# Attention on one Trainium2 core: GpSimd finishes q's rope ahead of k's, and makes the next head's lower weight parts in the waits of that order

## The chip, the cores and the metric

The kernel runs on one core of one Trainium2 chip. The metric is device time in microseconds (us) of one execution. The kernel before takes 2588.76 us, the median of three runs (2585.17 to 2589.17).

## The reference

The program is one transformer block in float32: a layer norm, an attention with three branches, a residual, and a feed-forward layer that routes 128 tokens per batch. The change lies in the attention, which is for each of 16 heads and 8 batches (512 tokens, head width 128):

```
q = (x @ Wq).reshape(b, n, H, HD)
k = (x @ Wk).reshape(b, n, H, HD)
v = (x @ Wv).reshape(b, n, H, HD)
q = _rope(q)
k = _rope(k)
...
return jnp.concatenate([t1 * cos - t2 * sin, t1 * sin + t2 * cos], axis=-1)
...
s_full = jnp.einsum('bnhd,bmhd->bhnm', q, k) * scale
```

The rope multiplies each half of q and k by a cosine and adds the other half times a signed sine. Compressed, selected and windowed softmax branches then share the scores of q and k.

## The kernel before

The attention (`attend`) goes through 128 units, one for a head and a batch; unit u is head u // 8 and batch u % 8. It is a software pipeline written by hand: in one pass of `body`, each engine projects unit u, scores unit u-1 and ends unit u-2 (the product of probabilities and v). Products keep float32 precision by splitting each operand into a high part (a copy rounded by ScalarE) and a low part (the difference), with three matmuls for one.

Every engine has one instruction stream in program order and waits on semaphores. In a unit:

- TensorE projects q and k (L479), scores the unit before (L505, L508), transposes probabilities (L521), projects v (L479 again), transposes v (L535) and multiplies by v (L546). Before it projects k it waits until ScalarE has copied the v of the unit before (`vt`) out of the bank that both share.
- ScalarE copies the projected q and k out of PSUM into `s_full` (L563), makes `pt_hi` (L579), then q's high part (L574), the exponentials of rows 3 and 2 (L585, L591), k's high part (L574), the exponentials of rows 1 and 0, and then `vt` (L563), `o_sb` (L625) and `v_hi` (L628). In the last unit of a head it also makes the high parts of the next head's weights (L134).
- SyncE stores `o_sb` (L405), and for q and then k swaps the two halves of `s_full` into `s_swap` with two DMAs (L396, L397). In the first unit of a head it also issues, behind that unit's store, the three weight loads of the next head (L130).
- GpSimd does the rope of q and k on 128x512 tiles. `turn_cos` (L440) is `s_full` times cosine, into `cosed`, once the copy is there. `turn_sin` waits for both swap DMAs, multiplies `s_swap` by sine (L445) and adds `cosed` and `s_swap` into `s_full` (L448). `low` (L452) takes the low part, once ScalarE has made the high part. The weights' low parts (L138) are made in the same stream, in the last unit of each head.
- VectorE reads score rows, works out the softmax coefficients and mixes the branches.

The inner loop `with eng.Fori(0, B - 1)` runs seven of a head's units; the unit with the weight split is written out ahead of it.

Of the kernel before, what the change touches and what calls it, by code (L numbers as in the profile page):

```python
# [84 lines left out]
def f32(ap):  # L85

    return ap.bitcast(F32)
# [215 lines left out]
def attend(nc, phase, banks, m, gates, xt_hi, xt_lo, weights, rope_d, o_dram, chunks):  # L303
# [68 lines left out]
    def steps(eng, body, start=lambda h: None, spare=lambda: None):  # L372


        start(0)
        body(0, 0, True, False, False, False)
        body(1, 1, True, True, False, False)
        with eng.Fori(2, B - 1) as b:
            body(b, b, True, True, True, False)
        with eng.Fori(1, H) as h:  # L380
            body(h * B - 1, B - 1, True, True, True, h)
            start(h)
            with eng.Fori(0, B - 1) as b:
                body(h * B + b, b, True, True, True, False)
        body(H * B - 1, B - 1, True, True, True, False)
        body(H * B, None, False, True, True, False)
        spare()
        body(H * B + 1, None, False, False, True, False)

    with nc.Block() as block:  # L390
# [45 lines left out]
        @block.gpsimd  # L436
        def _(pool):
            def turn_cos(u, k):
                pool.wait_ge(evacuated[k], u + 1)
                nc.gpsimd.tensor_tensor(cosed[k][:], s_full[k][:], rope[:, 0, :], ALU.mult).then_inc(cos_done[k], 1)  # L440

            def turn_sin(u, k):

                pool.wait_ge(swapped[k], u * 32 + 32)
                nc.gpsimd.tensor_tensor(s_swap[k][:], s_swap[k][:], rope[:, 1, :], ALU.mult).then_inc(sin_done[k], 1)  # L445
                pool.wait_ge(cos_done[k], u + 1)
                pool.wait_ge(sin_done[k], u + 1)
                nc.gpsimd.tensor_tensor(s_full[k][:], cosed[k][:], s_swap[k][:], ALU.add).then_inc(roped[k], 1)  # L448

            def low(u, k):  # L450
                pool.wait_ge(hi_done[k], u + 1)
                nc.gpsimd.tensor_tensor(qk_lo[k][:], s_full[k][:], f32(qk_hi[k][:]), ALU.subtract).then_inc(lo_done[k], 1)  # L452

            def body(u, b, project, score, end, split):
                if project:
                    for k in range(2):
                        turn_cos(u, k)
                        if split is not False:
                            weights.low(pool, nc.gpsimd, split, k)
                    for part in (turn_sin, low):  # L460
                        for k in range(2):
                            part(u, k)
                    if split is not False:
                        weights.low(pool, nc.gpsimd, split, 2)

            nc.gpsimd.memset(o_sb[:], 0.0).then_inc(out_slot_free, 16)
            nc.gpsimd.memset(shift1[:], 0.0).then_inc(out_evacuated, 1)
            pool.wait_ge(rope_loaded, 16)
            steps(pool, body, spare=lambda: chunks.low(pool, 0, 0, 1))

        @block.tensor
# [973 lines left out]
```

## Time and profile before

| what | value |
|---|---|
| median of three runs | 2588.76 us |
| the profiled execution's own time | 2585.8 us |
| its span, from first to last instruction | 2584.0 us |
| mean granted TensorE clock, as a share of full | 0.980 |
| TensorE busy (share of the span) | 2453.7 us (95%) |
| VectorE | 1843.8 us (71%) |
| GpSimd | 1590.1 us (62%) |
| ScalarE | 1412.9 us (55%) |

A busy share is an average over stages. The attention takes roughly the stretch from 120 us to 1965 us. What an order of instructions does there shows in the timeline of each engine: the start of one instruction minus the start of the one before it is the pace at which they follow, and brackets give how long the engine was idle before it and what ended that.

### The profile page before, as it was taken

The numbers are of one execution on the slowest core, as the hardware profiler recorded it, in microseconds if no ns is written. First come the engines' busy times: TensorE is split into PE (matmuls) and PEld (weight loads), VectorE is DVE, ScalarE is ACT, GpSimd is POOL, SyncE is SP. The second block draws the span as 40 slices with busy tenths as digits, with TensorE's granted clock in tenths as the row PEclk, the third lists the DMA queues.
The fourth block names the chain that finished last, engine by engine and source line by source line (L and its number), as shares of the span: only waits on it lengthen the run. The fifth ranks groups of instructions, "written<-read, shape, count | busy, mean of one in ns | idle before, by whom it ended". The sixth has DMA issues, their size and how long they took to land. (4 is left out here: it accounts for less than half of the span.)

```text
span 2584.0 us, 48592 instructions
## 1 busy us (share of the span) xinstructions
PE 2453.7 (95%) x12944; PEld 2082.9 (81%) x12944; DVE 1843.8 (71%) x5891; ACT 1412.9 (55%) x3810; POOL 1590.1 (62%) x1177
## 2 busy tenths in 40 slices
PE   5799999999999999999999999999996999999998
PEld 4688888888888888888888888888885888887776
DVE  6378888787787888778788878778883566566134
ACT  6466666666665666566666666656663222222442
POOL 0367777777777777677777767777762343343442
PEclk9899999999999999999999999999998999999999
DMA  3222222221212121222222222121215343342366
GB/s 119 65 53 66 61 61 61 61 73 49 71 50 72 50 73 53 69 61 61 61 61 64 57 64 70 50 70 50 61 53 178 118 143 125 119 146 70 103 179 208
DMA packets 145629, 211.74 MB, mean 82 GB/s; under 512 B 14912, under 2 KB 56128, under 8 KB 144576
## 3 DMA queue, kind: packets, MB, share of 16 engines
q1 hardware_dynamic: 145600, 211.37, 27.6%
q8 instruction: 16, 0.26, 0.0%
q14 instruction: 13, 0.11, 0.0%
HBM read 93.87 MB, written 50.33 MB: 56 GB/s over the span
## 5 line engine op out<-in xcount | busy, mean ns | idle before, releaser
L479 PE MATMUL bank<-xt_hi,w_hi 128*128 (+1 forms) x1536 | 630.4, 410 | 43.8 <-ACT vt L563 40.0
L479 PE MATMUL bank<-xt_hi,w_lo 128*128 (+1 forms) x1536 | 607.6, 396 | 0.0
L479 PE MATMUL bank<-xt_lo,w_hi 128*128 (+1 forms) x1536 | 605.3, 394 | 0.0
L440 POOL TENSOR_TENSOR cosed<-s_full,rope 128x512 f32<-128x512 f32 x256 | 329.8, 1291 | 371.1 <-ACT s_full L563 369.5
L479 PEld LDWEIGHTS bank<-xt_hi,w_hi 128*128 128x128 f32 x1536 | 293.1, 191 | 108.9 <-ACT vt L563 46.7
L641 DVE TENSOR_REDUCE shift<-bank 128x1 f32<-128x512 f32 (+3 forms) x512 | 247.9, 484 | 158.7 <-PE bank L508 158.7
L448 POOL TENSOR_TENSOR s_full<-cosed,s_swap 128x512 f32<-128x512 f32 x256 | 331.2, 1294 | 36.7
L445 POOL TENSOR_TENSOR s_swap<-s_swap,rope 128x512 f32<-128x512 f32 x256 | 329.4, 1287 | 39.2 <-DMA s_swap<-s_full 39.2
L479 PEld LDWEIGHTS bank<-xt_hi,w_lo 128*128 128x128 f32 x1536 | 292.4, 190 | 66.6
L479 PEld LDWEIGHTS bank<-xt_lo,w_hi 128*128 128x128 f32 x1536 | 293.9, 191 | 52.7
L452 POOL TENSOR_TENSOR qk_lo<-s_full,qk_hi 128x512 fp32r<-128x512 f32 x256 | 324.8, 1291 | 0.3 <-ACT qk_hi L574 0.3
L579 ACT ACTIVATE pt_hi<-bank 128x384 fp32r<-128x384 f32 (+1 forms) x384 | 174.6, 528 | 250.2 <-PE bank L521 250.2
L791 POOL TENSOR_TENSOR o_lo<-o_raw,o_hi 128x2048 fp32r<-128x2048 f32 x32 | 147.2, 4601 | 254.2 <-ACT o_hi L902 204.5
L563 ACT ACTIVATE s_full<-bank 128x512 f32<-128x512 f32 x256 | 154.5, 603 | 262.0 <-PE bank L479 261.8
L574 ACT ACTIVATE qk_hi<-s_full 128x512 fp32r<-128x512 f32 x256 | 160.4, 626 | 171.9 <-POOL s_full L448 171.9
L645 DVE TENSOR_REDUCE bank<-bank 128x8 f32<-128x512 f32 (+3 forms) x512 | 253.2, 495 | 0.0
L585 ACT ACTIVATE bank<-bank,shift 128x512 f32<-128x512 f32 (+3 forms) x512 | 251.3, 491 | 1.1 <-DVE bank L645 1.0
L591 ACT ACTIVATE win<-win,shift 128x192 f32<-128x192 f32 (+1 forms) x512 | 222.9, 435 | 0.0
L964 PE MATMUL bank<-wo_hi,o_hi 128*128 128x512 f32 x512 | 204.9, 400 | 6.1 <-PEq L390 3.3
L658 DVE SCALAR_TENSOR_TENSOR bank<-bank,coef,cb 128x192 f32<-128x192 f32 (+1 forms) x512 | 206.9, 404 | 0.0
L650 DVE TENSOR_TENSOR pt_lo<-bank,pt_hi 128x384 fp32r<-128x384 f32 (+1 forms) x384 | 206.2, 593 | 0.9 <-ACT pt_hi L579 0.8
L674 DVE SCALAR_TENSOR_TENSOR probs<-win,coef,bank 128x192 f32<-128x192 f32 (+1 forms) x512 | 199.9, 390 | 4.5
(164 smaller groups left out, 5429.2 us busy)
## 6 DMA issues: line engine op xcount, KB each, us to landing
s_swap<-s_full SPq DMA_DIRECT2D x512, 128.0 KB, 2.3
o_scratch<-o_sb SPq DMA_DIRECT2D x128, 256.0 KB, 2.0
o_raw<-o_scratch SPq DMA_DIRECT2D x32, 1024.0 KB, 6.4
xin<-in_L_attn_x SPq DMA_DIRECT2D x16, 1024.0 KB, 5.4
w_raw<-in_L_ffn_W SPq DMA_DIRECT2D x64, 256.0 KB, 3.1
base_scratch<-x SPq DMA_DIRECT2D x8, 1024.0 KB, 4.7
base<-base_scratch SPq DMA_DIRECT2D x32, 256.0 KB, 4.3
out<-base SPq DMA_DIRECT2D x32, 256.0 KB, 2.6
```

Source lines behind the costliest of these rows:

```text
L440: nc.gpsimd.tensor_tensor(cosed[k][:], s_full[k][:], rope[:, 0, :], ALU.mult).then_inc(cos_done[k], 1)
L445: nc.gpsimd.tensor_tensor(s_swap[k][:], s_swap[k][:], rope[:, 1, :], ALU.mult).then_inc(sin_done[k], 1)
L448: nc.gpsimd.tensor_tensor(s_full[k][:], cosed[k][:], s_swap[k][:], ALU.add).then_inc(roped[k], 1)
L452: nc.gpsimd.tensor_tensor(qk_lo[k][:], s_full[k][:], f32(qk_hi[k][:]), ALU.subtract).then_inc(lo_done[k], 1)
L479: last = nc.tensor.matmul(banks[QB[k]][:, :], w[k][:, c, :], v[:, bass.ds(b, 1), c, :], start=(n == 0), stop=(n == 3 * C - 1))
L585: nc.scalar.activation(n, n, ACT.Exp, bias=shift1[:, t:t + 1], scale=-1.0, accum_out=sums[:, 1, t:t + 1]).then_inc(exp_row, 1)
L591: nc.scalar.activation(win[:, t, lo:], win[:, t, lo:], ACT.Exp, bias=shift2[:, t:t + 1], scale=-1.0, accum_out=sums[:, 2, t:t + 1]).then_i ...
L641: nc.vector.tensor_reduce(shift1[:, t:t + 1], n[:, 0:(t + 1) * P], AX.X, ALU.min)
L645: nc.vector.reduce_sum(sc[:, t, 0:nb], n[:, 0:nb * BS].rearrange("p (n s) -> p n s", s=BS), AX.X).then_inc(row_read, 1)
L650: nc.vector.tensor_tensor(pt_lo[:, PTOFF[g]:PTOFF[g] + w], banks[(6, 7, 4)[g]][:, 0:w], f32(pt_hi[:, PTOFF[g]:PTOFF[g] + w]), ALU.subtract ...
L658: return nc.vector.scalar_tensor_tensor(out=to.rearrange("p (n s) -> p n s", s=BS), in0=e, scalar=coef[:, 1, t:t + 1], in1=cb[:, t, b0:b1] ...
L964: last = nc.tensor.matmul(banks[t][:, :], o[k % 2][:, g, t * P:(t + 1) * P], w[:, k * G + g, :], start=(k == 0 and n == 0), stop=(k == K - ...
```

## The change

GpSimd's stream within a unit is written in another order. Before: cosine of q, cosine of k, then sine and sum of q, sine and sum of k, then the two low parts. Now: cosine, sine and sum of q, then cosine, sine and sum of k, then the low parts. Where the next head's weights are split, the low part of Wq stays behind q's cosine, and that of Wk moves from behind k's cosine to behind k's sum. No instruction is added or removed, and no other engine's order changes.

```diff
             def body(u, b, project, score, end, split):
                 if project:
-                    for k in range(2):
-                        turn_cos(u, k)
-                        if split is not False:
-                            weights.low(pool, nc.gpsimd, split, k)
-                    for part in (turn_sin, low):
-                        for k in range(2):
-                            part(u, k)
+                    turn_cos(u, 0)
+                    if split is not False:
+                        weights.low(pool, nc.gpsimd, split, 0)
+                    turn_sin(u, 0)
+                    turn_cos(u, 1)
+                    turn_sin(u, 1)
+                    if split is not False:
+                        weights.low(pool, nc.gpsimd, split, 1)
+                    low(u, 0)
+                    low(u, 1)
                     if split is not False:
                         weights.low(pool, nc.gpsimd, split, 2)
```

GpSimd's stream in the inner loop, which seven of a head's eight units run (`cosed_900`, `s_swap_894` and `s_full_892` are q's, `cosed_901`, `s_swap_895` and `s_full_893` are k's; the ISA row is a drain of the engine):

```order
 L440 TENSOR_TENSOR cosed_900<-s_full_892,rope 128x512
-L440 TENSOR_TENSOR cosed_901<-s_full_893,rope 128x512
 L444 ISA
 L445 TENSOR_TENSOR s_swap_894<-s_swap_894,rope 128x512
 L448 TENSOR_TENSOR s_full_892<-cosed_900,s_swap_894 128x512
+L440 TENSOR_TENSOR cosed_901<-s_full_893,rope 128x512
 L445 TENSOR_TENSOR s_swap_895<-s_swap_895,rope 128x512
 L448 TENSOR_TENSOR s_full_893<-cosed_901,s_swap_895 128x512
```

k's cosine has moved from ahead of q's sine to between q's sum and k's sine.

GpSimd's stream in the last unit of a head, where the next head's weights are split (`w_lo_59` is the low part of Wq, `w_lo_60` that of Wk, `qk_lo_898` and `qk_lo_899` those of q and k):

```order
 L138 TENSOR_TENSOR w_lo_59<-w_raw_53,w_hi_56 128x512
-L440 TENSOR_TENSOR cosed_901<-s_full_893,rope 128x512
-L138 TENSOR_TENSOR w_lo_60<-w_raw_54,w_hi_57 128x512
 L444 ISA
 L445 TENSOR_TENSOR s_swap_894<-s_swap_894,rope 128x512
 L448 TENSOR_TENSOR s_full_892<-cosed_900,s_swap_894 128x512
+L440 TENSOR_TENSOR cosed_901<-s_full_893,rope 128x512
 L445 TENSOR_TENSOR s_swap_895<-s_swap_895,rope 128x512
 L448 TENSOR_TENSOR s_full_893<-cosed_901,s_swap_895 128x512
+L138 TENSOR_TENSOR w_lo_60<-w_raw_54,w_hi_57 128x512
 L452 TENSOR_TENSOR qk_lo_898<-s_full_892,qk_hi_896 128x512
 L452 TENSOR_TENSOR qk_lo_899<-s_full_893,qk_hi_897 128x512
```

Two instructions that stood ahead of q's sine now stand behind q's sum, and one of the two, the weights' low part, behind k's sum as well.

## Rows read from the trace of the kernel before

**Rows 1.** The page's busy times: us, share of the span, instructions.
```profile
PE 2453.7 (95%) x12944; PEld 2082.9 (81%) x12944; DVE 1843.8 (71%) x5891; ACT 1412.9 (55%) x3810; POOL 1590.1 (62%) x1177
```
**Rows 2.** Who waited for whom, 150 to 1900 us: total us, times, longest.
```profile
ACT qk_hi L574 <- POOL s_full L448: 159.5, 123, 4.0
...
POOL s_swap L445 <- DMA s_swap<-s_full: 38.7, 14, 3.1
PE bank L479 <- ACT vt L563: 34.5, 29, 2.4
```
**Rows 3.** TensorE's timeline: start, duration, instruction; starts of units, one wait.
```profile
214.30 0.45 PE L479 MATMUL bank<-xt_hi,w_hi 128*128 x1
...
1014.21 0.45 PE L479 MATMUL bank<-xt_hi,w_hi 128*128 x1
...
1017.62 0.50 PE L479 MATMUL bank<-xt_hi,w_hi 128*128 x1 [0.45 <-ACT vt L563]
...
1028.82 0.45 PE L479 MATMUL bank<-xt_hi,w_hi 128*128 x1
...
1060.48 0.45 PE L479 MATMUL bank<-xt_hi,w_hi 128*128 x1
...
1074.31 0.45 PE L479 MATMUL bank<-xt_hi,w_hi 128*128 x1
...
1818.99 0.45 PE L479 MATMUL bank<-xt_hi,w_hi 128*128 x1
```
**Rows 4.** GpSimd's timeline in a unit of the inner loop.
```profile
1066.87 1.29 POOL L440 TENSOR_TENSOR cosed<-s_full,rope 128x512 f32<-128x512 f32 x1 [1.43 <-ACT s_full L563]
1068.12 1.27 POOL L445 TENSOR_TENSOR s_swap<-s_swap,rope 128x512 f32<-128x512 f32 x1
1069.54 1.30 POOL L448 TENSOR_TENSOR s_full<-cosed,s_swap 128x512 f32<-128x512 f32 x1
1070.80 1.29 POOL L445 TENSOR_TENSOR s_swap<-s_swap,rope 128x512 f32<-128x512 f32 x1
1072.23 1.29 POOL L448 TENSOR_TENSOR s_full<-cosed,s_swap 128x512 f32<-128x512 f32 x1
```
**Rows 5.** ScalarE's timeline in the same unit.
```profile
1063.48 0.60 ACT L563 ACTIVATE s_full<-bank 128x512 f32<-128x512 f32 x1
...
1073.63 0.62 ACT L574 ACTIVATE qk_hi<-s_full 128x512 fp32r<-128x512 f32 x1
...
1075.84 0.60 ACT L563 ACTIVATE vt<-bank 128x512 f32<-128x512 f32 x1
1076.32 0.61 ACT L625 ACTIVATE o_sb<-bank 128x512 f32<-128x512 f32 x1
1076.80 0.62 ACT L628 ACTIVATE v_hi<-bank 128x512 fp32r<-128x512 f32 x1
```
**Rows 6.** SyncE's timeline there, and the swaps' time from issue to landing.
```profile
1064.78 0.59 SPq L397 DMA_DIRECT2D s_swap<-s_full  x1
...
DMA to landing us min/median/max: 2.2/2.3/2.4
```
**Rows 7.** ScalarE's timeline around a weight split.
```profile
1012.12 0.63 ACT L574 ACTIVATE qk_hi<-s_full 128x512 fp32r<-128x512 f32 x1 [2.06 <-POOL s_full L448]
...
1018.40 0.66 ACT L134 ACTIVATE w_hi<-w_raw 128x512 fp32r<-128x512 f32 x1
1018.92 0.63 ACT L563 ACTIVATE s_full<-bank 128x512 f32<-128x512 f32 x1
```
**Rows 8.** Timelines of ScalarE and GpSimd behind a weight load.
```profile
1031.99 0.63 ACT L563 ACTIVATE s_full<-bank 128x512 f32<-128x512 f32 x1
...
1039.35 1.29 POOL L445 TENSOR_TENSOR s_swap<-s_swap,rope 128x512 f32<-128x512 f32 x1 [2.84 <-DMA s_swap<-s_full]
...
1048.47 0.63 ACT L563 ACTIVATE s_full<-bank 128x512 f32<-128x512 f32 x1
```
**Rows 9.** A window after that: engines' busy us, granted PE clock, DMA.
```profile
1047.00:1053.00 6.00, 5.31 (x18) 4.29 (x19) 4.97 (x18) 2.70 (x7) 1.51 (x2) 0.72 0.30 87
```

## The prediction

> **What bounds the kernel now.** I read the page first, then the table of waits over the attention, then each engine's timeline in one ordinary unit, in a unit with a weight split and in one behind a weight load. TensorE is busy 95% of the span and GpSimd 62% [rows 1], so by averages GpSimd's order should not matter. TensorE starts an ordinary unit every 13.83 us (1060.48 to 1074.31) with no wait in it; but from the first split unit to the last, fourteen heads apart (214.30 to 1818.99), a head takes 114.62 us, which is 3.98 us more than 8 x 13.83 = 110.64 [rows 3]. These 4 us have two places, both at the same wait: TensorE wants to project k and ScalarE has not yet copied v out (`vt`), 29 times and 34.5 us in all [rows 2].
>
> The first place is the split unit. ScalarE waits 2.06 us for q's rope, which stands behind two weight low parts on GpSimd [rows 7]; `vt` is late and TensorE stands still for 0.45 us by the row. From unit start to unit start this is 14.61 us (1014.21 to 1028.82), 0.78 above 13.83 [rows 3]. The second is the unit behind a weight load, with the other 3.98 - 0.78 = 3.2 us of a head. There GpSimd waits for q's swap DMA, which stands behind three weight loads in the queue, 14 times and 38.7 us [rows 2]: q's sine starts at 1039.35, 7.36 us after the copy of q at 1031.99 [rows 8]. TensorE's clock then falls: 0.72 of full as a mean over 6 us, so part of that stretch is at 1.2 GHz instead of 2.4 [rows 9].
>
> **The change in an ordinary unit.** What the reader must look for is a loop that comes back to itself one unit later: ScalarE copies q out, the swap DMAs run, GpSimd turns q and k, ScalarE makes k's high part, its last exponentials, `vt`, `o_sb`, `v_hi`, and only then copies the next q out. If this loop takes longer than 13.83 us it becomes the bound, whatever the busy shares say. Its steps, by start to start:
>
> - Copy of q (1063.48, rows 5) to issue of the second swap DMA (1064.78, rows 6): 1.30. To its landing: 2.4, the longest of 2.2 to 2.4 [rows 6], as it is the second of two in one queue. To q's sine some 0.05, my estimate. The sine could start at about 1067.23, that is 3.75 us after the copy; before, it starts at 1068.12, since k's cosine stands in front of it and that waits for k's copy [rows 4].
> - q's sine to q's sum 1.42 (1068.12 to 1069.54); q's sum to the next instruction 1.26; k's cosine to the next 1.25 (1066.87 to 1068.12); k's sine to k's sum 1.43 (1070.80 to 1072.23) [rows 4].
> - k's sum to k's high part 1.40 (1072.23 to 1073.63, rows 4 and 5); high part to `vt` 2.21; `vt` to `o_sb` 0.48; to `v_hi` 0.48; to the next copy of q, another 0.48 as between such copies [rows 5].
>
> The loop as it will be: 3.75 + 1.42 + 1.26 + 1.25 + 1.43 + 1.40 + 2.21 + 3 x 0.48 = 14.16 us; I take 14.1, since the landing may be 2.3. A second way to it: sine of q 0.89 us sooner (1068.12 to 1067.23), k's cosine 1.25 us added behind it, 13.83 + 0.36 = 14.19. So q's rope is done 0.9 us sooner, which nobody needs: ScalarE waits for it 1.3 us a unit (159.5 over 123, rows 2), but `vt` hangs on k's high part further down its stream. And k's rope is done about 0.3 us later, which TensorE does feel, each unit. Bounds of the loop: with a landing of 2.2 and every rounding in its favour 13.9, with a landing of 2.5 and a dearer restart 14.25.
>
> **The change in the four kinds of unit of a head**, counted from copy of q to copy of q:
>
> - Split unit: GpSimd has the low part of Wq in the wait for the swap (the swap is ready 3.75 us after the copy's start, while cosine and low part take 2 x 1.25 from the copy's end at 0.6): free. That of Wk is behind k's sum; low q and low k come one instruction later, and TensorE scores them only after 24 matmuls more, the next q and k: free, and 1.25 us if that cover were gone. ScalarE's extra w_hi pushes the next copy of q by 0.52 (1018.40 to 1018.92, rows 7). 14.1 + 0.5 = 14.6. The 0.78 us wait that TensorE had here is gone as such, but the loop's pace takes its place.
> - First unit of a head: 14.1. GpSimd's third weight part is in the wait for the swap.
> - Behind the load: 7.36 in place of 3.75 up to q's sine [rows 8], so 14.1 + 3.6 = 17.7. Where before k's cosine was done while GpSimd waited for the DMA, it now comes after, and k's rope ends 1.25 us later than it did.
> - Next one: TensorE has stood over 3 us and its clock falls, as in most heads before. Copy to copy took 15.0 with the clock low (1048.47 to 1063.48, rows 8 and 5). 15.0.
> - The four left: 4 x 14.1 = 56.4.
>
> A head: 14.6 + 14.1 + 17.7 + 15.0 + 56.4 = 117.8 us against 114.62, so 3.2 us more, and 14 of them 44.5 us. Five units ahead of the first split unit at 0.27 and eight or so behind the last give 3 us. The end of the attention and the later stages do not change. Sum: 2585.8 + 47.5 = 2633 us against the profiled execution's own time; that execution lies 3 us under the median of the runs, so a median of 2633 to 2636; I say 2632, since the first units of a head have bits of slack that I rounded away.
>
> **A rule on the clock.** By the row above, TensorE fell to a mean of 0.72 of its clock after it had waited for `vt` behind a weight load [rows 9]; the other waits of 0.45 us did nothing of the kind, as the ordinary unit at 13.83 behind the split shows [rows 3]. The Trainium skill, TensorE: Matmul & The Clock Gate, in Part 1 (The HAM clock gate), says that the gate follows how busy the engine has been lately and that its phase runs free of the kernel. That would let the fall come in some heads and stay out in others, and let a longer stand catch more; by it the sum could be one fall in each head, as I have it, or two. No row here shows a stand as long as the one I expect.
>
> **The rivals.**
>
> - *The loop stays below 13.83 us.* For it: my sum is over by 0.3 us only, from ten steps, and the landing is rounded. Against: each step has a row, nothing in it is a guess but 0.05. Then ordinary units stay at 13.83, the split units give 15 x 0.78 = 11.7 us back, and the units behind a load lose 14 x 1.25 = 17.5, and with a clock fall in the heads that escaped it some 8 more (waits: 34.5 - 15 x 0.45 = 27.8 us over 14 heads, so 2.0 a head of the 3.2; the rest of some 1.2 is restart and clock, where a full fall costs about 1.6). That gives 2600 to 2604.
> - *Faster.* One mechanism: behind the load, q's sine may start sooner. `o_sb` releases the store and the loads in front of the swap; if ScalarE, freed of its wait for q, had `o_sb` out sooner, and the queue were clear 1.25 us sooner, k's cosine would cost nothing there and the 11.7 us of the split units would remain: 2577. It turns at 11.7 / 14 = 0.84 us a head, which the queue would have to give back. Against it: `vt` and `o_sb` follow k's high part, not q's, and k's rope is not sooner. It also needs the first rival.
> - *More clock.* The stand behind the load grows from about 2.2 to 3.5 us. If it costs two falls, or if the small stand that each ordinary unit now has brings falls of its own, another 1.6 us a head or more: 2655.
> - *No change.* The loop at 13.9 and no new falls of the clock would be +0.6 us a head, 10 us with both ends, 2599; for nothing at all the terms would have to cancel.
>
> **Chances.** The forecast (loop of 14.0 to 14.2, one fall) 0.76; loop below the bound or just at it 0.10; more clock 0.07; faster 0.03; no change 0.04. The range of 2604 to 2650 takes the ends of the loop (13.95 and 14.2, each 0.1 to 0.15 away from 14.1 over 126 units, 13 to 19 us) and leaves the low rivals and most of the clock's out. Changes under 0.2% can't be told from none here. Faster by more 0.03, within 0.04, slower 0.93.
>
> **What would show it.** Right: TensorE's waits for `vt` go from 29 to over 100; ordinary units are 14.0 to 14.2 apart and even; GpSimd waits for the swap DMA in nearly every unit (1.8 us: q's cosine is done some 1.9 us after the copy starts, the sine comes at 3.75) and no longer for the copy of k; ScalarE's wait for q's rope all but goes, and it waits for k's instead; behind the load the unit is about 1.2 us longer than before and the clock falls in nearly every head. Wrong: ordinary units at 13.83 with the waits for `vt` only at the head's turn, or swaps that land in under 2.1 us, or a `vt` that comes less than 2 us after k's high part.

## The result, and the profile after

The changed kernel takes 2626.54 us, the median of four runs (2624.17 to 2630.85), against 2588.44 for the kernel before (2585.17 to 2589.17). The ratio is 1.0149, with a 95% interval of 1.0137 to 1.0161: it is slower by 38 us. The forecast was 2632, in a range of 2604 to 2650. The profiled execution has a span of 2626.2 us, 42.2 above the 2584.0 of before.

The page of the changed kernel, busy times and two of its costliest groups (us busy, mean ns, then the engine's idle time ahead of them and what ended it; TensorE's and ScalarE's lines stand three lines lower in the file than before):

```profile
PE 2475.4 (94%) x12944; PEld 2085.5 (79%) x12944; DVE 1843.9 (70%) x5891; ACT 1428.9 (54%) x3810; POOL 1589.8 (61%) x1177
...
L445 POOL TENSOR_TENSOR s_swap<-s_swap,rope 128x512 f32<-128x512 f32 x256 | 328.9, 1285 | 244.8 <-DMA s_swap<-s_full 244.8
L440 POOL TENSOR_TENSOR cosed<-s_full,rope 128x512 f32<-128x512 f32 x256 | 330.9, 1292 | 221.2 <-ACT s_full L566 221.2
```

GpSimd does the same work in the same time (1590.1 before, [rows 1]), and it still idles 39% of the span. Only what it waits for has changed. The table of waits over the attention, 150 to 1940 us (the one of before stops at 1900, as its attention ends earlier):

```profile
POOL s_swap L445 <- DMA s_swap<-s_full: 236.0, 128, 5.8
...
ACT qk_hi L577 <- POOL s_full L448: 148.4, 181, 4.3
...
PEld bank L482 <- ACT vt L566: 84.2, 80, 4.3
PE bank L482 <- ACT vt L566: 53.6, 29, 3.9
```

Against [rows 2]: GpSimd waits for the swap DMA 128 times and no longer 14 times, and TensorE's 29 listed waits for `vt` have grown from 34.5 to 53.6 us. That the number is still 29 must not be read as "ordinary units do not wait", nor as "the same 29": 14 of them lay between the copies of q of the split and the first unit and now lie one unit later, and 14 are behind the load in both kernels. The row of TensorE's own weight loads (PEld) has 80, and TensorE's timeline in an ordinary unit shows the small stand that the list leaves out:

```profile
1129.04 0.39 PE L482 MATMUL bank<-xt_lo,w_hi 128*128 x1
1129.27 0.39 PE L482 MATMUL bank<-xt_hi,w_lo 128*128 x1
1129.55 0.50 PE L482 MATMUL bank<-xt_hi,w_hi 128*128 x1
```

Matmuls follow each other at 0.23 us; here the first of k's projection comes after 0.28 and then fills the pipeline anew (0.34 to the next). The loop that the prediction worked out is in the timelines of GpSimd, ScalarE and SyncE, an ordinary unit from copy of q (1116.31) to copy of q (1130.33), 14.02 us:

```profile
1117.01 1.28 POOL L440 TENSOR_TENSOR cosed<-s_full,rope 128x512 f32<-128x512 f32 x1 [1.90 <-ACT s_full L566]
1119.99 1.28 POOL L445 TENSOR_TENSOR s_swap<-s_swap,rope 128x512 f32<-128x512 f32 x1 [1.70 <-DMA s_swap<-s_full]
1121.42 1.30 POOL L448 TENSOR_TENSOR s_full<-cosed,s_swap 128x512 f32<-128x512 f32 x1
1122.67 1.30 POOL L440 TENSOR_TENSOR cosed<-s_full,rope 128x512 f32<-128x512 f32 x1
1123.93 1.28 POOL L445 TENSOR_TENSOR s_swap<-s_swap,rope 128x512 f32<-128x512 f32 x1
1125.35 1.29 POOL L448 TENSOR_TENSOR s_full<-cosed,s_swap 128x512 f32<-128x512 f32 x1
```
```profile
1116.31 0.63 ACT L566 ACTIVATE s_full<-bank 128x512 f32<-128x512 f32 x1
...
1126.67 0.63 ACT L577 ACTIVATE qk_hi<-s_full 128x512 fp32r<-128x512 f32 x1 [0.56 <-POOL s_full L448]
...
1128.90 0.59 ACT L566 ACTIVATE vt<-bank 128x512 f32<-128x512 f32 x1
...
1130.33 0.62 ACT L566 ACTIVATE s_full<-bank 128x512 f32<-128x512 f32 x1
```
```profile
1117.61 0.59 SPq L397 DMA_DIRECT2D s_swap<-s_full  x1
```

Follow it: copy of q, second swap issued 1.30 us later, q's sine 3.68 after the copy, then 1.43, 1.25, 1.26 and 1.42 on GpSimd, 1.32 to k's high part, 2.23 to `vt`, 1.43 to the next copy. No step waits for TensorE. In [rows 4], the same q's sine had k's cosine ahead of it, and that cosine waited for TensorE's projection of k: before, the engines on this ring were paced by TensorE, now TensorE is paced by the ring.

Behind the weight load GpSimd, ScalarE and TensorE show (three timelines, then a window of TensorE's clock):

```profile
1061.91 1.29 POOL L445 TENSOR_TENSOR s_swap<-s_swap,rope 128x512 f32<-128x512 f32 x1 [5.37 <-DMA s_swap<-s_full]
```
```profile
1054.56 0.62 ACT L566 ACTIVATE s_full<-bank 128x512 f32<-128x512 f32 x1
...
1072.24 0.62 ACT L566 ACTIVATE s_full<-bank 128x512 f32<-128x512 f32 x1
```
```profile
1071.45 0.80 PE L482 MATMUL bank<-xt_hi,w_hi 128*128 x1 [3.55 <-ACT vt L566]
```
```profile
1071.00:1077.00 6.00, 5.55 (x15) 4.39 (x15) 4.76 (x17) 1.88 (x5) 2.28 (x2) 0.51 0.30 87
```

The sine still starts 7.35 us after the copy, as in [rows 8], but k's cosine now follows, and the two copies lie 17.68 us apart where they were 16.48. TensorE stands 3.55 us, and the granted clock is 0.51 over the next 6 us, practically all at 1.2 GHz, where [rows 9] had 0.72.

### The profile page after: what moved, and what is told of

Read it like the earlier page. It is cut to its first block and busy times, and to the rows that moved or that the text cites. A ratio compares the mean times of both kernels' runs of the same rounds, so it can differ in the third digit from the quotient of the medians.

```text
span 2626.2 us, 48592 instructions
## 1 busy us (share of the span) xinstructions
PE 2475.4 (94%) x12944; PEld 2085.5 (79%) x12944; DVE 1843.9 (70%) x5891; ACT 1428.9 (54%) x3810; POOL 1589.8 (61%) x1177
## 5 line engine op out<-in xcount | busy, mean ns | idle before, releaser
L482 PE MATMUL bank<-xt_hi,w_hi 128*128 (+1 forms) x1536 | 640.5, 417 | 62.7 <-ACT vt L566 57.8
```

Of the source, the lines that this page charges most:

```text
L482: last = nc.tensor.matmul(banks[QB[k]][:, :], w[k][:, c, :], v[:, bass.ds(b, 1), c, :], start=(n == 0), stop=(n == 3 * C - 1))
```

## The experiments

Ten kernels were run. This table reads the same thing from each trace, the starts of ScalarE's copy of q: the mean distance to the next one, over the fourteen heads that have a weight load, by the kind of unit in which it begins. TensorE's own work is 13.83.

| kernel | median us | split | first | behind load | next | ordinary (mean of 4) | head |
|---|---|---|---|---|---|---|---|
| before | 2588.4 | 15.46 | 13.07 | 16.39 | 14.29 | 13.85 | 114.62 |
| changed | 2626.5 | 14.72 | 13.91 | 17.67 | 15.21 | 14.06 | 117.73 |
| split_only | 2564.5 | 14.67 | 13.06 | 16.49 | 13.73 | 13.85 | 113.36 |
| load_only | 2617.0 | 15.46 | 13.07 | 17.64 | 15.20 | 13.85 | 116.78 |
| ord_only | 2609.9 | 15.33 | 13.92 | 16.36 | 14.32 | 14.06 | 116.19 |
| not_load | 2605.9 | 14.76 | 13.91 | 16.49 | 14.63 | 14.06 | 116.04 |
| late_old | 2543.9 | 15.44 | 13.06 | 13.64 | 13.83 | 13.85 | 111.39 |
| late_new | 2549.8 | 14.71 | 13.93 | 13.94 | 13.94 | 13.94 | 112.29 |
| late_split | 2532.8 | 14.53 | 13.10 | 13.82 | 13.83 | 13.85 | 110.69 |
| khigh_new | 2572.4 | 14.46 | 13.24 | 16.52 | 14.40 | 13.83 | 113.96 |
| dup_new | 2674.3 | 15.00 | 14.48 | 17.68 | 15.26 | 14.48 | 120.35 |
| dup_old | 2608.5 | 15.86 | 13.59 | 16.48 | 14.88 | 13.83 | 116.14 |

**Where the new order costs: four kernels with it in one place or all but one.** GpSimd's units of a head are written apart, and each takes the old or the new order:

```diff
+                with pool.Fori(1, H) as h:
+                    body(h * B - 1, B - 1, True, True, True, h, SPLIT_NEW)
+                    body(h * B, 0, True, True, True, False, ORD_NEW)
+                    body(h * B + 1, 1, True, True, True, False, LOAD_NEW)
+                    with pool.Fori(2, B - 1) as b:
+                        body(h * B + b, b, True, True, True, False, ORD_NEW)
```

split_only. 

> GpSimd's new order in the last unit of a head alone, where the next head's weights are split; the old order in all others. The loop theory (the new order makes the way from one copy of q to the next 14.06 us in every ordinary unit, above TensorE's 13.83, and sets the pace): with ordinary units untouched the 0.78 us that TensorE loses behind each of 15 split units is gained, 2575 to 2580 us. The rival (the cost sits at the head's turn, in the split unit and the unit behind the weight load): at or above the kernel before, 2588 us or more.

Measured: 2564.46, a ratio of 0.9908 (0.9878 to 0.9939), 23 us faster than before. The split and first units together lose 0.80 us a head, the expected gain. Behind the load it is 0.10 more. The rest, 0.56 a head less, is in the unit next to that: its mean falls from 14.29 to 13.73 because TensorE's clock fell in 3 heads of 14 and not in 8. The expected range took no account of the clock. The part that the order itself explains is 14 x 0.80 = 11 us; that fewer falls are more than chance is likely, since all five runs have a mean granted clock of 0.983 to 0.986, where fifteen of the kernel before beside them have 0.977 to 0.986, but it is not shown. A further 3.9 us of the profiled spans' difference (2562.0 against 2584.0) lie ahead of the first split unit, where both kernels have the old order.

load_only. 

> The new order in the unit behind the weight load alone. Both theories: k's cosine runs after the late swap instead of during it, k's rope ends 1.25 us later, 14 times 1.25 = 17.5 us, and up to 9 us more where TensorE's clock now falls in heads that had escaped it: 2606 to 2615 us. If the head's turn alone made the change slow, this kernel would come near the changed one, 2620 us or more.

Measured: 2617.04, a ratio of 1.0108 (1.0069 to 1.0147), 30 us slower than the runs of before beside it (2587.3). Behind the load 1.25 us more, as expected to the hundredth; next to it 0.91 more, for the clock now falls in all fourteen heads. That term was 9 us in the expectation and 13 here, since in three heads the low stretch was twice as long. So this one place comes nearer to the whole change than expected, but not to it.

ord_only. 

> The new order in the ordinary units alone, the old one in the split unit and behind the weight load. The loop theory: six units a head go from 13.83 to about 14.06 us from copy to copy of q, and what the first unit of a head used to catch up (13.07 us there) is no longer caught up; a head of 117.1 us against 114.6, 14 times 2.5 = 35 us, so 2615 to 2626 us. The rival (head's turn only): 2588 to 2593 us.

Measured: 2609.88, a ratio of 1.0082 (1.0057 to 1.0108), 23 us slower. The rival that only the head's turn matters falls: ordinary units went to 14.06, and the first unit to 13.92. It is 5 us under the expected range: a head lost 1.57 us and not 2.5. That is 0.84 in the four ordinary units and 0.85 in the first, but 0.13 gained in the split unit and nothing lost behind the load and next to it (16.36 and 14.32), where the clock fell in 3 heads and not 8.

not_load. 

> The changed kernel with the old order in the unit behind the weight load. The loop theory: 1.25 us a head comes back there, with some of the second falls of the clock, 14 times 1.0 to 1.5 us below the changed kernel: 2605 to 2614 us, still clearly slower than before. The rival (head's turn only): 2580 to 2590 us.

Measured: 2605.93, a ratio of 1.0069 (1.0048 to 1.0089). Taking the new order out behind the load gives back 1.18 us there and 0.58 next to it (the medians differ by 21 us), and the kernel is still slower than before.

**The late swap taken away.** SyncE issues the weight loads behind the next unit's swaps instead of ahead of them, with the old order, the new one, and the new one in the split unit alone:

```diff
                 body(second, 0, True, True, True)
+                swap(second + 1, 0)
+                swap(second + 1, 1)
                 if not (isinstance(h, int) and h == H - 1):
                     weights.load(sp, h + 1)
-                with sp.Fori(1, B - 1) as b:
+                body(second + 1, 1, False, True, True)
+                with sp.Fori(2, B - 1) as b:
```

late_old. 

> The kernel before, with SyncE issuing the next head's weight loads behind the next unit's two swaps instead of ahead of them. No swap stands behind the loads, so the unit behind the load is an ordinary one and TensorE's clock does not fall there: 14 heads times 3.2 us less, 2539 to 2547 us.

Measured: 2543.93, a ratio of 0.9827 (0.9810 to 0.9843). The 3.2 us a head behind the load are gone, with every fall of the clock between the first and the last split.

late_new. 

> The changed kernel with the same late loads. The loop theory: a head is 14.7 + 13.9 + 6 times 14.06 = 113.0 us with no late swap and no fall of the clock in it, about 22 us over the kernel before with late loads (111.4 a head), so 2557 to 2568 us. The rival (only the head's turn makes the new order slow): with the late swap gone the new order is no slower, at or below the kernel before with late loads.

Measured: 2549.81, a ratio of 0.9848 (0.9831 to 0.9864), 6 us over late_old and not 22. Its sign is as the loop has it, its size is not: ordinary units came at 13.94 and not at 14.06. Even that would be 0.90 us a head, 12.6 us; the profiled execution is the slowest of the four (2553.95, the others 2548.45 to 2550.42), so the usual one is likely to be nearer still to late_old. SyncE's and ScalarE's rows in this kernel, against the 1.30 us of the changed one:

```profile
948.31 0.62 ACT L569 ACTIVATE s_full<-bank 128x512 f32<-128x512 f32 x1
...
962.21 0.63 ACT L569 ACTIVATE s_full<-bank 128x512 f32<-128x512 f32 x1
```
```profile
949.47 0.59 SPq L397 DMA_DIRECT2D s_swap<-s_full  x1
```

The second swap leaves 1.16 us after the copy, so 0.14 less, and the loop is shorter by just about that (13.90 here, 13.94 in the mean). The changed kernel has both distances in itself. In the units that SyncE's inner loop runs in the fourteen heads, the swap leaves 1.30 us after the copy and the next copy comes after 14.06; in the last head, with the same order on every engine, it is 1.16 and 13.89 to 13.97 (here 13.94):

```profile
1877.83 0.62 ACT L566 ACTIVATE s_full<-bank 128x512 f32<-128x512 f32 x1
...
1891.77 0.62 ACT L566 ACTIVATE s_full<-bank 128x512 f32<-128x512 f32 x1
```
```profile
1878.99 0.60 SPq L397 DMA_DIRECT2D s_swap<-s_full  x1
```

What makes SyncE issue sooner in one place than in the other was not tried.

late_split. 

> Late loads, and the new order in the last unit of a head alone. TensorE waits at neither place of a head, 110.7 to 111 us each: 8 to 11 us below the kernel before with late loads, 2530 to 2537 us, and below both kernels.

Measured: 2532.81, a ratio of 0.9782 (0.9766 to 0.9798): the fastest of all, 56 us under the kernel before. A head takes 110.69 us of 110.64 that TensorE needs. In the table of waits from 150 to 1900 us TensorE is left with one for `vt`:

```profile
PEld bank L511 <- ACT vt L595: 0.5, 1, 0.5
```

**The loop shortened.** ScalarE makes k's high part behind all exponentials, in the changed kernel:

```diff
-                if project:
-                    high(u, 1)
                 if score:
                     exp_of_row(u, 1)
...
                     exp_of_window(u, 0)
                 if project:
+                    high(u, 1)
                     if score:
```

khigh_new. 

> The changed kernel with ScalarE making k's high part behind all exponentials of the unit instead of between them, so that only 0.5 us and not 2.2 lies between it and the copy of v. The loop theory: the loop is shorter by about 0.4 us in an ordinary unit (the exponentials then set it), so these go back to TensorE's 13.83, and 1.7 us shorter behind the load: 2565 to 2595 us. If k's rope is not on the way that sets the pace, the time stays within 5 us of the changed kernel.

Measured: 2572.39, a ratio of 0.9939 (0.9922 to 0.9955), 54 us under the changed kernel with GpSimd's order untouched. Ordinary units are back at 13.83. Its ScalarE rows:

```profile
996.18 0.62 ACT L577 ACTIVATE qk_hi<-s_full 128x512 fp32r<-128x512 f32 x1
996.70 0.58 ACT L566 ACTIVATE vt<-bank 128x512 f32<-128x512 f32 x1
997.18 0.60 ACT L627 ACTIVATE o_sb<-bank 128x512 f32<-128x512 f32 x1
997.66 0.60 ACT L630 ACTIVATE v_hi<-bank 128x512 fp32r<-128x512 f32 x1
998.13 0.62 ACT L566 ACTIVATE s_full<-bank 128x512 f32<-128x512 f32 x1
```

From k's high part to `vt` it is 0.52 us and no longer 2.21 to 2.23, and the high part has no wait for k's rope in brackets: the ring is no longer closed there. The kernel before with the same move on ScalarE was not run, so what the earlier exponentials do by themselves at the head's turn is not separated; in ordinary units they can't have done more, as these take 13.85 there already.

**The loop lengthened.** One more copy on ScalarE behind `v_hi`, of a constant tile into a tile that nothing reads:

```diff
+                    act.wait_ge(extra_done, u)
+                    nc.scalar.activation(extra[:], rope[:, 0, :], ACT.Copy).then_inc(extra_done, 1)
```

dup_new. 

> The changed kernel with one more copy of a 128x512 tile on ScalarE behind v_hi in every unit (0.5 us; its output is used by nothing). The loop theory: ScalarE's copy of v_hi and what follows lie on the loop that sets the pace, so all 0.5 us show in each of some 125 units: 55 to 70 us above the changed kernel. If TensorE, or something off this loop, set the pace of ordinary units, under 20 us.

Measured: 2674.34, a ratio to before of 1.0333 (1.0307 to 1.0358), 48 us above the changed kernel. The expectation was 55 to 70, so the dose came out too small. In its ordinary units:

```profile
1168.19 0.66 ACT L636 ACTIVATE extra<-rope 128x512 f32<-128x512 f32 x1
1168.71 0.62 ACT L569 ACTIVATE s_full<-bank 128x512 f32<-128x512 f32 x1
```
```profile
1169.90 0.58 SPq L400 DMA_DIRECT2D s_swap<-s_full  x1
```

The extra copy takes 0.52 us on the ring, but the second swap now leaves 1.19 us after the copy of q in place of 1.30, so 14.06 + 0.52 - 0.11 = 14.47, as measured (14.48). Behind the load the dose costs nothing (17.68 against 17.67). There the swap does not hang on the copy of q but on the store of `o_sb` and the three loads ahead of it. Store and second swap, in the changed kernel (copy of q at 1054.56) and in this one (copy of q at 1078.87):

```profile
1054.38 0.34 SPq L405 DMA_DIRECT2D o_scratch<-o_sb  x1
...
1057.27 0.59 SPq L397 DMA_DIRECT2D s_swap<-s_full  x1
```
```profile
1078.17 0.34 SPq L408 DMA_DIRECT2D o_scratch<-o_sb  x1
...
1081.06 0.59 SPq L400 DMA_DIRECT2D s_swap<-s_full  x1
```

From store to swap it is 2.89 us in both. The extra copy stands between `o_sb` and the copy of q, so it only shortens the wait behind it: q's sine starts 6.84 us after the copy, as a mean of the fourteen heads, and not 7.34.

dup_old. 

> The kernel before with the same extra copy. The loop theory: its loop has about 0.9 us to spare at q's sine, so ordinary units stay at 13.83; only the split unit and the one behind the weight load take 0.5 us each, with a fall of the clock or two more: 7 to 22 us above the kernel before, a third or less of what the changed kernel pays.

Measured: 2608.51, a ratio of 1.0080 (1.0055 to 1.0105), 20 us slower than before. Ordinary units stay at 13.83 with the same 0.52 us added; the loss is 0.92 in the split and first units, and 0.6 next to the load, where the clock falls in every head. An equal dose costs the changed kernel 2.6 us a head and the kernel before 1.5, and none of the latter in ordinary units. The range held, but "a third or less of what the changed kernel pays" did not (20 of 48 us), for the changed kernel pays less than expected, and the clock falls in six heads more.

## Why the prediction was right

The forecast, the loop above TensorE's pace, held, and by its own steps (us a head, [rows 3] to [rows 8] against the table):

| step | predicted | measured |
|---|---|---|
| split unit | 14.6 | 14.72 |
| first unit | 14.1 | 13.91 |
| behind the load | 17.7 | 17.67 |
| next | 15.0 | 15.21 |
| four ordinary | 56.4 | 56.23 |
| head | 117.8 | 117.73 |

That the head agrees within 0.1 us is in part luck: the first unit came 0.2 us under its step and the one next to the load 0.2 over. The first unit is shorter because SyncE issues the second swap 1.16 us after the copy there and not 1.30, so that q's sine comes after 3.58 us in the mean and not after 3.72. The upper end of the range follows from the stated 13 to 19 us about the loop; the lower one (2604, 28 us down) lies 9 us below what they give, and the working does not say why.

A head is 3.11 us longer: 1.28 behind the load, 0.92 next to it, 0.84 in the four ordinary units and 0.10 in the split and first unit. The last figure answers the question what became of the stall that the change removes. The split unit is shorter by 0.74, but the first unit of a head, which used to catch up (13.07), can't do so on a ring of 13.9 us and gives 0.84 back. Only where ordinary units stay below TensorE's pace is the gain real, as split_only shows.

- *The loop's length.* 14.16 by the sum, taken as 14.1, measured 14.05 to 14.08 in most ordinary units. Each step agrees within 0.1 us. In the unit shown the two largest differences are q's sine, 3.68 after the copy and not 3.75, and k's high part, 1.32 after k's sum and not 1.40. khigh_new shortens this ring and dup_new lengthens it, with GpSimd's order untouched, and the pace follows; dup_old has the same dose and its ordinary units stay at 13.83; and the changed kernel's own last head has a swap 0.14 us sooner and a pace 0.12 us faster. Together they show it.
- *k's cosine behind the late swap.* 1.25 predicted, 1.28 measured, and 1.25 with that place alone (load_only).
- *The clock.* One fall a head was assumed. The granted clock shows 13 low stretches with 61 us in fourteen heads, against 8 with 27 us before: none in one head, and five twice as long. The Trainium skill, TensorE: Matmul & The Clock Gate, Part 1 (The HAM clock gate), says that the gate's phase runs free of the kernel; the trace agrees so far as some heads escape and others catch more at nearly the same stand (none after 3.60 us, 6.8 us at half clock after 3.71). The rival of more clock was half right in kind and small in size (15.21 for 15.0); ordinary units had no fall.
- *The ends.* Predicted 3 us slower, measured 1.4 us faster: up to the first split unit the changed kernel is 2.3 us ahead (a start-up unit of 13.97 us where there were 16.45), behind the last it loses about 0.9. This term missed its sign, as far as the runs show by the luck of the clock and not by the order: up to the first split unit the three profiled kernels with the old order there and the present loads and ScalarE order (before, split_only, load_only) take 203.5, 199.7 and 199.8 us, and the three with the new one (changed, not_load, ord_only) 201.2, 201.1 and 205.6. The two long ones have, from 130 or 132 us on, a stretch of 6.8 us at half clock; the others have 3.4 us or nothing there. The four start-up units behind that take 13.90 to 13.95 where they took 13.83 to 13.91, and those of the last head 13.89 to 13.97, so the 0.27 us a unit of the prediction was about three times too much. The ends together with heads of 43.6 us make the 42.2 of the span, where the prediction had 47.5.
- *ScalarE's wait for q's rope.* The prediction put it at 1.3 us a unit and nearly gone afterwards. The row that it read takes q and k and all kinds of unit together: in the ordinary units of the fourteen heads it was 0.79 us and is 0.17, with 0.43 for k's where there was none. Over all units it has halved (169.9 to 87.3 us) and not gone, for behind the load it stays long (3.96 us at 1064.75). Nothing in the sum hangs on it.
- *TensorE's count of waits.* The prediction named over 100 listed waits as the sign; the list has 29 for matmuls and 80 for weight loads. The stand in an ordinary unit is too short to be listed as a wait of a matmul. The distance of units was the sign to go by.

Of the rivals, a loop below the bound, a faster kernel and no change all fell with the 14.06 us of ordinary units. That ordinary units carry a good part of the loss is shown by ord_only (23 us alone). The single places do not add up (-23, +30 and +23 make 30, the change 38). In the traces split_only and ord_only make -1.26 + 1.57 = 0.31 us a head, and not_load, which has both places, 1.42. Of the 1.11 between them 0.87 are next to the load, where the clock falls in 7 heads and not in 3, and 0.22 in the split and first unit, where the gain needs slack that the new order takes away.

## What to carry to other kernels

An engine that is idle 39% of the time can still set the pace, if its work lies on a ring that comes back to itself in the next iteration: add up start to start all the way round, DMA landing included, and compare with the busiest engine's period before moving anything onto it. In an in-order stream, a wait for an early event (q's swap) placed ahead of work that was ready sooner puts that work on the ring; here it cost 1.25 us where 0.9 was spare. And a reordering that helps in one kind of unit should be made in that kind alone: with the weight loads moved behind the swaps besides, the same edit is part of the fastest kernel here.

## What the runs showed of the hardware

- SyncE issues the second of two swap DMAs 1.30 us after the copy of q starts in the ordinary units of the changed kernel's fourteen heads, but 1.16 in the first unit of each head, in its last head and in late_new, with the same instructions and waits on SyncE; in dup_new, where its store leaves 0.68 us before the copy and not 0.17, it is 1.19. Why is open. On a ring, these 0.1 us show in full in the period (14.06 against 13.94).
- A swap DMA that SyncE issues behind a store and three weight loads leaves 2.89 to 2.91 us after the store, whether the copy that it reads is early or late (changed kernel and dup_new).
- A stand of TensorE of 3.55 us was followed by 6 us at a mean granted clock of 0.51; one of 2.08 us by a mean of 0.72 [rows 9]. The length of the stand alone does not decide: behind the load, stands of 1.99 to 2.71 us in dup_old were followed by a stretch at half clock in 14 heads of 14, those of 1.42 to 2.69 in khigh_new in 6, and those of 1.69 to 2.46 in split_only in 3.
- GpSimd's rope instructions on 128x512 float32 take 1.26 to 1.32 us each in the changed kernel, 1.28 in the mean where VectorE is idle beside them and 1.29 where it is busy.
